# Weight fetches between row scatters, three token sums on TensorE, and a later expert split in a fused attention and mixture-of-experts kernel

## The reference

```
x = x + tanh(g_xattn[0]) * cross_attention_0(ctx, norm(x), mask)
x = x + tanh(g_ffn[0])   * ternary_mlp(norm(x))
x = x + tanh(g_xattn[1]) * cross_attention_1(norm(x), ctx)    # 16 heads of 64, 1024 keys
h = norm(x)
scores = sigmoid(h @ gate_w.T)                                # 16 experts in 4 groups
tidx   = top 4 of scores + bias, inside the 2 best groups
w      = 2.5 * scores[tidx] / sum(scores[tidx])
y      = sum over 4 chosen e of w_e * (silu(h @ w1[e].T) * (h @ w3[e].T)) @ w2[e].T
shared = (silu(h @ ws1.T) * (h @ ws3.T)) @ ws2.T
x = x + tanh(g_ffn[1]) * (y + shared)
```

## Time and profile before

| | us |
|---|---|
| median of 3 runs | 1132.21 |
| the profiled execution: its time | 1131.97 |
| its span, first to last instruction | 1130.1 |
| PE / DVE / ACT / POOL busy | 981.3 / 826.2 / 702.4 / 444.5 |
| first attention and ternary MLP, until about | 470 |
| attention blocks, until about | 935 |
| routing and shared expert, until the first row load | 994.4 |
| expert tiles, until the last down product | 1104.7 |
| last scatters, loads, sums and stores | 1130.1 |

### The profile page before, as it was taken

How to read it: one execution, slowest core, us unless ns; L and a number is a source line. 1 busy time by engine, 2 the same in 40 slices (tenths; PEclk the granted TensorE clock), 3 DMA queues, 4 the chain that set the end, 5 groups by cost and what they waited for, 6 DMA issues and landing times. The chain is left out here.

```text
span 1130.1 us, 19254 instructions
## 1 busy us (share of the span) xinstructions
PE 981.3 (87%) x6532; PEld 868.4 (77%) x6532; DVE 826.2 (73%) x1712; ACT 702.4 (62%) x1368; POOL 444.5 (39%) x489
## 2 busy tenths in 40 slices
PE   1789979899799989999898999989899987759990
PEld 1668868688588778888797988879798777559990
DVE  6687774777632369788888978888897876646765
ACT  3477756776552468777677767867777672125650
POOL 5154441644147713342404333151423424634441
PEclk9889989999899999999999999999999997869996
DMA  4100000000311202948312824031220476277435
GB/s 133 33 1 1 1 5 1 1 1 1 117 31 41 74 24 80 256 147 225 118 61 71 248 59 155 1 116 26 70 71 18 129 272 249 90 268 231 128 105 204
DMA packets 78255, 109.20 MB, mean 97 GB/s; under 512 B 16496, under 2 KB 62704, under 8 KB 75600
## 3 DMA queue, kind: packets, MB, share of 16 engines
q1 hardware_dynamic: 72064, 76.37, 22.9%
q0 software_dynamic: 6096, 31.61, 7.7%
HBM read 57.27 MB, written 50.68 MB: 96 GB/s over the span
## 5 line engine op out<-in xcount | busy, mean ns | idle before, releaser
L344 PE MATMUL PS<-R 128*128 128x512 f32 (+3 forms) x2669 | 576.5, 360 | 49.2 <-DVE R L1927 14.4
L344 PEld LDWEIGHTS PS<-R 128*128 128x128 f32 x2669 | 430.8, 196 | 106.4 <-issue 19.0
L1718 DVE TENSOR_TENSOR R<-PS,R 128x512 fp32r<-128x512 f32 x320 | 205.4, 684 | 39.6 <-ACT R L1388 38.7
L1388 ACT ACTIVATE R<-PS 128x512 fp32r<-128x512 f32 x320 | 174.7, 595 | 79.6 <-PE PS L841 78.4
L1351 ACT ACTIVATE FA<-PS,nmax 128x1024 f32<-128x1024 f32 (+1 forms) x160 | 192.5, 1203 | 42.8 <-DVE nmax L1707 26.9
L854 PE MATMUL PS<-R 128*128 128x256 f32 x1408 | 202.6, 290 | 11.9 <-DVE FB L1726 10.6
L841 PE MATMUL PS<-eye,FA 128*128 128x128 f32 x1408 | 185.7, 276 | 11.5 <-DVE R L1718 4.2
L841 PEld LDWEIGHTS PS<-eye,FA 128*128 128x128 f32 x1408 | 160.9, 141 | 44.3 <-issue 19.3
L854 PEld LDWEIGHTS PS<-R 128*128 128x128 f32 x1408 | 178.8, 190 | 20.1 <-issue 17.2
L1707 DVE TENSOR_REDUCE nmax<-PS 128x1 f32<-128x1024 f32 x128 | 155.6, 1221 | 32.5 <-PE PS L344 22.0
L532 POOL TENSOR_SCALAR R<-R 64x512 fp32r<-64x512 f32 x40 | 26.0, 650 | 236.5 <-ACT R L1503 175.4
(11 more groups left out here) (254 smaller groups left out, 1276.4 us busy)
## 6 DMA issues: line engine op xcount, KB each, us to landing
R<-split POOLq DMA_DIRECT2D x16, 1280.0 KB, 8.4
rows<-FA SPq DMA_DIRECT2D x3, 5869.5 KB, 25.3
split<-R SPq DMA_DIRECT2D x32, 512.0 KB, 3.2
FA<-rows SPq DMA_DIRECT2D x47, 136.5 KB, 2.4
wst<-w_in SPq DMA_DIRECT2D x4, 1024.0 KB, 5.0
FB<-we_in SPq DMA_DIRECT2D x16, 256.0 KB, 4.0
split<-R SPq DMA_DIRECT2D x16, 256.0 KB, 2.5
FB<-k_in SPq DMA_DIRECT2D x16, 128.0 KB, 2.0
```

Source lines behind the costliest of these rows:

```text
L344: last = mm(out, a, b, start=(n == 0), stop=(n == len(passes) - 1), skip_group_check=skip)
L1388: a_(L.pt[0][:, (u // 2) % 2, 4 * g_:4 * g_ + 4, (u % 2) * P:(u % 2) * P + P], L.turn(u, g_).rearrange("p (t n) -> p t n", t=4), ACT.Copy) ...
L1718: inc(v.tensor_tensor(lo, turned, hi.bitcast(F32), ALU.subtract), "p_lo")
```

## The change

Five edits are made together.

1. GpSimd waits for `at_lo` (the end of `out_lo`) before each pair of `presplit` at a block's end.
2. In the last block `choose_experts`, `mark_chosen` and `number_rows` of the first chunk go behind `out_lo`, `find_slots(0)` goes behind `out_add`, and `rank(0)`, `down(0)` and the DVE and ACT parts of job 0 move back; job 3 moves forward on DVE, and `gate_up(3)` goes ahead of `down(2)`. TensorE gets 24 products with a zero operand (`busy`) behind the shared expert.
3. Experts 9 and 10 are fetched ahead of the 13th and the 15th scatter of chunk 1, and the last four scatters wait for `e_y` 4.
4. Experts 11 and 12 are fetched ahead of the result scatters of tiles 4 and 6 (before: both ahead of tile 1), expert 15 ahead of tile 8 as before, and expert 14 ahead of tile 10 (before: ahead of tile 0). Experts 14 and 15 now are one group.
5. The sums of token tiles 1, 3 and 5 are made on TensorE, as products of diagonal weight matrices (made by ACT in iterations 28 to 39) with the loaded parts. 36 zero products stand ahead of them. DVE adds each sum to `x` in one instruction.

```diff
-FETCHED = ((0, 1, 2), (3, 4, 5), (6, 7, 8, 13, 14), (9, 10), (11, 12), (15,))
+FETCHED = ((0, 1, 2), (3, 4, 5), (6, 7, 8, 13), (9, 10), (11, 12), (14, 15))
...
             copy_queries(L1, 2 * i + 1, (28 * i - 14 + 1, 28 * i - 14 + 4))
             pair1_low(2 * i + 1, 28 * i - 14 + 5)
+            pool.wait_ge(s["at_lo"], 4 * i + 2)
             presplit(4 * i - 2)
...
             for t in range(t0, t0 + n):
+                if t == NT - 1:
+                    pool.wait_ge(s["e_y"], 4)
                 for k in range(4):
                     i = 4 * t + k
+                    if i in (4 * NT - 4, 4 * NT - 2):
+                        fetch_expert(9 if k == 0 else 10)
...
-        pool.wait_ge(s["wo_done"], 4 + 4 * NG1)
-        fetch_expert(14)
         pool.wait_ge(s["e_y"], 4)
         pool.wait_ge(s["got3"], 16)
-        for e in (9, 10):
-            fetch_expert(e)
         for j in range(TILES):
             r = j % RINGS
-            if j == 1:
-                for e in (11, 12):
-                    fetch_expert(e)
+            if j in (4, 6):
+                fetch_expert(9 + j // 2)
             if j == 8:
                 pool.wait_ge(s["y_done"], 8)
                 fetch_expert(15)
+            if j == 10:
+                pool.wait_ge(s["wo_done"], 4 + 4 * NG1)
+                fetch_expert(14)
...
+        def busy(bank):
+            return mm(PS[:, bank, :], zero, R[:, 7680:8192], start=True, stop=True, skip_group_check=True)
...
-        rank(0)
         gate_up(0, 0, 0)
         out_project(L1, 1, last_block)
+        rank(0)
         for n in range(4):
             zero_banks(4)
             zero_banks(5)
-        down(0, 0, 0)
         pe.wait_ge(s["x_att"], 4 + 4 * NG1)
         ln_turn(4 * NB + 2, LN_BANKS[1], late1)
         router(1)
+        down(0, 0, 0)
...
         down(1, 1, 0)
+        gate_up(3, 1, 1)
         down(2, 0, 1)
-        gate_up(3, 1, 1)
         down(3, 1, 1)
+        pe.wait_ge(s["e_full"], 4)
+        for n in range(24):
+            busy(2 + n % 2)
...
+        for n in range(36):
+            mm(PS[:, 4, :], zero, R[:, 7680:8192], start=True, stop=True, skip_group_check=True)
+        pe.wait_ge(s["diag_set"], 12)
+        for i, t in enumerate(PE_SUMS):
+            pe.wait_ge(s[f"got{t}"], 16 * len(range(t, TILES, HELD)) + 16)
+            for k in range(4):
+                last = mm(PS[:, i, 0:256], diag[4 * i + k], back[t][:, D * k:D * k + D], start=(k == 0), stop=(k == 3))
+            last.then_inc(s["part_sum"], 1)
...
+        def share_matrix(i):
+            if i == 0:
+                act.wait_ge(s["weighted"], 1)
+                act.wait_ge(s["y_done"], 16)
+            c = 4 * PE_SUMS[i // 4] + i % 4
+            a_(diag[i], eye[:, :], ACT.Copy, scale=weight[:, c:c + 1]).then_inc(s["diag_set"], 1)
...
             attention(L1, b, C, fill)
             if not more:
                 out_norm(L1, C)
                 out_lo(L1, b, C)
-                find_slots(0)
+                choose_experts(0)
+                mark_chosen(0)
+                number_rows(0)
                 return
...
-        job(0, 0)
-        out_add(L1, 1, 2 * NG1 + 1, (0,))
-        job_low(0, 0)
-        out_add(L1, 1, 2 * NG1 + 1, (1,))
+        out_add(L1, 1, 2 * NG1 + 1)
+        find_slots(0)
         dve.wait_ge(s["x_att"], 4 + 4 * NG1)
         norm(4 * NB + 2, x_tiles(1), late1)
         split_norm(3 * NB + 2, 1)
         find_weights(0)
+        job(0, 0)
+        job_low(0, 0)
...
         for t in range(NT):
+            if t in PE_SUMS:
+                i = PE_SUMS.index(t)
+                dve.wait_ge(s["part_sum"], i + 1)
+                inc(v.tensor_tensor(x[:, t, :], PS[:, i, 0:256], x[:, t, :], ALU.add), "out_ready")
+                continue
```

More of the change, by code:

```diff
@@ L93 @@
 HELD = 8
+PE_SUMS = (1, 3, 5)
 SPARE_ROWS = NB * S * 4
 CHUNKS = ((0, 4), (4, 4))
-FETCHED = ((0, 1, 2), (3, 4, 5), (6, 7, 8, 13, 14), (9, 10), (11, 12), (15,))
+FETCHED = ((0, 1, 2), (3, 4, 5), (6, 7, 8, 13), (9, 10), (11, 12), (14, 15))
 FETCHED_IN = {e: i for i, group in enumerate(FETCHED) for e in group}
@@ L281, in program @@
                  + [FB[:, ROW * i:ROW * (i + 1)] for i in range(3)] + [FA[:, 3072:3072 + ROW]])
+    diag = ([RT[:, P * i:P * i + P] for i in range(6)] + [xs[:, P * i:P * i + P] for i in range(4)]
+            + [bo[:, P * i:P * i + P] for i in range(2)])
     late0, late1 = ([t[:, 0:D] for t in row_tiles[4 * b:4 * b + 4]] for b in range(NB))
@@ L304, in program @@
         "fw0_ready fw1_ready f1_done f2_done f_act f_hi f_lo f3_done x_ffn ln_half fw2_ready "
-        "gw_split gate_done gate_sig part_set ew_split g_done u_done e_silu e_full e_hi e_lo e_y x_shared "
+        "gw_split gate_done gate_sig part_set diag_set part_sum ew_split g_done u_done e_silu e_full e_hi e_lo e_y x_shared "
         "consts preset filled taken_set ranked slots_set placed_rows0 placed_rows1 offsets_set "
@@ L693, in _ @@
             pair1_low(2 * i + 2, 28 * i + 5)
+            pool.wait_ge(s["at_lo"], 4 * i + 4)
             presplit(4 * i)
@@ L705, in _ @@
         pair1_low(2 * NG1 + 1, 28 * NG1 - 14 + 5)
+        pool.wait_ge(s["at_lo"], 4 * NG1 + 2)
         for e in range(4 * NG1 - 2, E):
@@ L1585, in _ @@
         job(0, 0)
-        job_hi(0, 0)
         ln_root(4 * NB + 2)
@@ L1589, in _ @@
         ln_split(3 * NB + 2, 1, LNH)
+        job_hi(0, 0)
         route_scores(1)
@@ L1629, in _ @@
                 rows_out(j - 2)
+            if 28 <= j < 40:
+                share_matrix(j - 28)
     @block.vector
@@ L2103, in fill @@
                     choose_groups(0)
-                    choose_experts(0)
-                    mark_chosen(0)
-                    number_rows(0)
             attention(L1, b, C, fill)
@@ L2133, in job @@
             dve.wait_ge(s["u_done"], j + 1)
+            if j == 3:
+                dve.wait_ge(s["e_lo"], 3)
             dve.wait_ge(s["e_silu"], j + 1)
@@ L2157, in _ @@
         job_low(2, 1)
+        job(3, 1)
+        job_low(3, 1)
         find_weights(1)
```

2 lines of the change are left out of this document (removed).

## The result

The change makes the kernel slower, by 0.3%. On one chip, 20 runs of each, the kernel before takes 1132.62 us (median; 1128.92 to 1137.58) and the changed one 1134.74 us (1131.80 to 1141.16). The ratio is 1.0026, with a 95% interval of 1.0015 to 1.0037. The forecast, 1127.1 us and faster, was wrong, and the range (1119 to 1133) missed the time by 1.7 us. The profiled execution of the changed kernel took 1133.98 us (span 1132.2, granted clock 0.964), 2.0 more than the one of before (1131.97, span 1130.1, clock 0.959), so the two traces show about the difference that the timing shows (0.26% of 1132.6 is 2.9).

A forecast was written before the change was run, and what follows sets the result against it. Bounds: routing, row scatters and loads, TensorE in the tile loop, final DVE sums. -8.3 - 1.5 - 2.0 + 7.7 + 2.0 - 2.8 = -4.9 us from 1131.97 gave 1127.1 us; range 1119 to 1133 for 8 in 10.

The forecast's parts named there:

- signs that were to prove me wrong: No idleness of TensorE at tile 14, or block periods still at 66.2 us.
- A: Stretch of six blocks from the first spreading of reciprocals on DVE; forecast -6.9 us, with 5 block ends.
- B: Stretch of the last block, to its spreading of reciprocals on DVE; forecast -1.4 us, with 1 block end.
- its term: Edit 2, routing: the second chunk's row scatters start at 968.5, 1.9 us earlier.
- C: Stretch to second chunk's first row scatter, forecast -1.9; as rival: block-end gain not passed on, 1135.4, chance 0.07.
- D: Stretch from there to first turned row, forecast +0.4; as rival: row scatters held up 3 us, 1130.1, chance 0.07.
- one end of my range: Second chunk's start: 967.3 with GpSimd still in chunk 0, or 970.4 with nothing gained.
- E: Stretch of the tile loop, from the first turned row to ACT's last result copy; forecast +7.7 us.
- the -2.0: Edit 4, tile loop: gain from removing ACT's stall for a `put` buffer at 1022.5 to 1024.08, -2.0 us.
- Rival B: Tile loop pays for late weights with the clock, stalls of 3.7 and 5.7 us: 1136.8 us, chance 0.07.
- rival E: At the end, loads of parts end last by more or TensorE's sums run late, nothing gained: 1129.9, chance 0.05.
- Rivals A: Rival A, tile loop: fetches land in time, stalls shrink to about 2 us, clock stays: 1119.4 us, chance 0.20.

The follow-up runs named there:

- experiment 1: Kernel before with edit 1 alone, GpSimd waiting for `at_lo` before each pair of expert splits: 1126.06 us, ratio 0.9946 to the kernel before.
- experiment 3: Changed kernel with GpSimd splitting the shared expert's weights only after DVE's norm in the last block: 1131.90 us, ratio 0.9994 to the kernel before.
- 6: Changed kernel with experts 11, 12, 14, 15 ahead of tiles 2, 4, 6, 8's scatters and shared expert's split behind DVE's norm: 1123.14 us, ratio 0.9916.
- experiment 7: Changed kernel with loop fetches earlier, shared expert's split behind DVE's norm, and experts 9 and 10 fetched behind the row scatters: 1117.73 us, ratio 0.9868.
- Experiment 8: Kernel of experiment 7 without edit 2, routing and shared expert in the old order, no 24 zero products: 1118.66 us, ratio 0.9880 to the kernel before.
- after: The changed kernel with all five edits, against the kernel before: 1134.74 us, ratio 1.0026.
- experiment 9: Changed kernel with experts 9 and 10 fetched right behind the last row scatter, without waiting for any row load: 1136.69 us, ratio 1.0040 to the kernel before.
- experiment 4: Changed kernel with experts 9 and 10 fetched behind the row scatters again, after the fourth row load: 1129.85 us, ratio 0.9981 to the kernel before.
- 5: Changed kernel with all eight token sums on DVE again, no diagonal matrices, no 36 zero products: 1137.52 us, ratio 1.0045 to the kernel before.

## Why the prediction was wrong, point by point

The signs that I had named came true: 1.29 us at the block ends, periods of 64.8, stalls at tiles 11 and 14, a low clock behind them. Only the first row load came at 992.86 instead of 987, and none of the signs that were to prove me wrong appeared. They all stood where I had looked; the largest part of the error did not.

**Edit 1: right in size, wrong in that nothing follows from it.** The six block ends gave 6 x 1.39, and experiment 1 shows the five of them in A alone. The step that failed is this sentence of edit 1: "None stands in the 8 us behind `out_lo`, so the sum is the same by it, and it only names what the edit could collide with." A collision 30 us further on cost what 8 us of looking could not show. I asked where the delayed GpSimd split would go. I did not ask what becomes of the other meetings of DVE and GpSimd once DVE's line of work is 9.3 us ahead and GpSimd's, which waits for loads, only 4.5. The distance that kept them apart before was 0.26 us (908.46 to 908.72), and it was in the trace. About 3.0 us of GpSimd's lag are edit 1's own doing, since its split now waits for DVE. The norm then took 4.25 to 4.93 us in every kernel that let the two meet, and 1.37 or 1.38 in the four that did not (experiments 3, 6, 7 and 8).

There was a second error in the same sentence. I looked for DVE operations "with two SBUF inputs"; the norm is a TENSOR_SCALAR with one. The Trainium skill (SBUF — State Buffer, Who interferes with whom) names both kinds: operations with two SBUF inputs, and copies or `tensor_scalar` in a mode that reads one tensor through both ports. The trace agrees, with 1.37 against 4.93 us. Its words that the other engine "fully blocks" fit as well: DVE's first instruction starts 0.18 us behind GpSimd's first subtraction, and its first three end at 901.24, 902.17 and 904.07, each about 0.15 us behind the end of a GpSimd instruction (901.10, 902.02 and 903.92). The fourth, with GpSimd done, takes 0.40.

B grew by 4.8 against its forecast. The mean of the seven kernels with the collision is 69.7, that of the four without it 67.3: 2.4 us for the collision, 3.0 in the pair of after and experiment 3. The remaining 1.5 are not explained by it. In all eleven kernels with edit 1 the clock was at its lower level for 3.4 or 6.8 us between 895 and 906, and in six of them for 3.4 more further on in the block (10.2 us of B in after, 3.4 in experiment 9, 6.8 in the others), where before shows 1.00. At 0.50 the four products take 2.08 instead of 1.09. That is enough for 1.5 us, but no run changed the clock alone, and with 6.8 us at the lower level B still lies anywhere from 68.8 to 70.3 with the collision. So this part is argued and not shown.

**Edit 2: its term was right by accident.** The second chunk starts 1.7 us earlier, for 1.9 forecast. But it also does so in experiment 1, which has no edit 2. Experiment 8, which drops it, loses 1.4 us in C and gets 0.8 back in D, and its time is not told from that of experiment 7. What sets the start in after is visible in the counts: the first scatter is issued at 942.5, the second chunk's at 964.2, and 16 times 1.36 is 21.8. GpSimd is at its bound, and the first scatter's later start, which edit 2 brings, eats what the rest of it gains. I had that as one end of my range.

**Edit 3: the step that failed is the landing of the last scatter, and what it is worth.** "Fetch 10 [...] 994.1; two more scatters: 995.0" forecast the first row 29.4 us behind the second chunk's start. It was 30.9, or 1.5 late, though the first row load itself took 2.22 (issued at 992.86) where I had 2.7. The term that was too small is the landing of the fetches: expert 9's took 7.06 us where I had put 5.8. Counted from the chunk's start, it landed at 23.5 us instead of 22.1, expert 10's at 27.4 instead of 25.6, and the last scatter at 28.4 instead of 26.5. The larger error is that I compared only with before. Against fetching behind the first rows (experiment 4) the placement costs 4.7 us, and the gain over before that I forecast is not there either (D is 1.65 longer than before). I wrote "but then no fetch is in the way of the first rows"; both ways of having 2.6 MB under way ahead of them (after, experiment 9) delay them against experiment 4, by 4.7 and 6.4 us.

**Edit 4: right mechanism, right places, size short by 1.1 us.** Forecast were waits of 2.9 and 4.8 us and half speed behind the second. There were 3.53 and 3.48, and the clock fell behind both (PEclk 0.83 in either stretch). The stall that went was taken for 2.0 us; experiment 1, which still has it, has an E of 104.95, and experiment 7, which has neither it nor the new ones, 104.15. So that gain is below 1 us. Against 104.15 the late fetches cost after 9.8 us, where I had 9.7 (7.7 of stalls and 2.0 of clock), so the mis-sized term of this edit is the -2.0. In experiments 4, 5 and 9 the two waits were 4.4 to 5.5 us each, and E was 1.7 to 3.5 us longer than in after. Rival B had this mechanism, and its decision point of 14.6 us of waits and low clock was not reached. The time came out on its side because of stretch B, which no rival had.

**Edit 5: right in size, nearly so in its path.** -2.3 for -2.8, and a load of parts sets it (8.10 us at 1115.51), but another one than forecast. It is the load of token tile 5, whose sum TensorE makes; DVE waits for that sum (2.01 us) and its addition before it starts the eight sums of tiles 6 and 7 at 1126.02, 1.0 us behind the landing of the load that I had taken as the last (1125.01). So a little of rival E was there.

Summed against the forecast: last block +4.8, edits 2 and 3 +1.5, edit 4 +1.1, edit 5 +0.5, the 470 us that no edit touches -1.0. No edit touches that start, and it lies anywhere from 466.8 to 471.6 in the profiles of these kernels, so part of the scatter of single times comes from it.

Rivals A, C and E did not happen: the fetches were late, the block gain was passed on (A 388.6 to 388.8 in all eleven kernels), and the end gained 2.3 us. D came true in kind, with 1.5 us instead of 3.

## What to carry to other kernels

When one engine is made faster over many rounds, write down how far each engine's line of work moves, and check every place where two of them came close before; a gap of 0.26 us is not a margin. Look for collisions as far as the shift lasts, not only beside the edit, and count a TENSOR_SCALAR on DVE that reads one fp32 tensor from SBUF, as the norm here, among those that can collide with GpSimd. Before large fetches are put in front of a wanted small load, price them against fetching behind it, and time two late fetches together: here the removal of the first wait lengthened the second from 3.48 to 7.48 us.

## What the runs showed of the hardware that was not expected

- Four TENSOR_SCALAR of 128x256 (one SBUF tensor in, fp32) on DVE take 1.37 us alone and 4.25 to 4.93 beside a GpSimd TENSOR_TENSOR of 128x768 that takes 1.8. The GpSimd side is not slowed (1.81 against 1.83).
- About the same idleness of TensorE had different outcomes for the clock: 2.45 us in the last block left PEclk at 1.00 before, 2.44 us at the same place took it to 0.50 after. In the loop, the six products behind a wait came at either level (experiment 3):

```profile
1020.12 1.30 PE L347 MATMUL PS<-R 128*128 x6 [2.90 <-DMA R<-split]
...
1031.46 2.28 PE L347 MATMUL PS<-R 128*128 x6 [4.43 <-DMA R<-split]
```

  Behind the wait of 3.53 in after the six took 1.31, and only the products behind them fell. My forecast set a sharp limit of idle time for the clock; these rows show none.
- A fetch of 1280 KB on the software queue landed 6.4 to 9.7 us after its issue in the chains of these kernels, depending on what else was under way. The first row load of 136.5 KB took 2.22 us in after, with the fetches landed, and 8.44 us in experiment 9 beside two such fetches on another queue.
